# First edge layer of a graph network: VectorE's order, and scatter-adds one group later

## The reference

```python
h  = relu(layernorm(x))
Wh = h @ W + b
Wr, Wc = Wh[row], Wh[col]                    # row = src, col = dst
dot = sum(Wr * Wc);  nr, nc = norms of Wr, Wc
sim = dot / max(nr * nc, EPS)
base = adj_v * sc * (row != col)
prop_pos = segment_sum((base * relu(sim))[:, None] * Wc, row)
prop_neg = segment_sum((base * -relu(-sim))[:, None] * Wc, row)
x = x + scale * (c0 * prop_pos + c1 * prop_neg + c2 * Wh)
```

## Time and profile before

| what | us |
|---|---|
| three runs | 2419.44, 2421.32, 2427.26 (median 2421.32) |
| the profiled execution | 2421.7 |
| its span | 2419.1 |
| GpSimd busy | 1689.1 (70%) |
| TensorE busy | 1563.3 (65%) |
| VectorE busy | 1546.1 (64%) |
| ScalarE busy | 864.6 (36%) |

### The profile page before, as it was taken

One profiled execution on the slowest core, in us unless ns is written; L12 is line 12 of the kernel. 1 busy time (PEld: TensorE's weight loads), 2 busy tenths in 40 slices (PEclk: granted clock), 3 DMA queues, 4 the chain that ended last, 5 costly groups with the idle time before them and its releaser, 6 DMA issues. The chain is left out here.

```text
span 2419.1 us, 57388 instructions
## 1 busy us (share of the span) xinstructions
PE 1563.3 (65%) x16004; PEld 1340.3 (55%) x16004; DVE 1546.1 (64%) x5636; ACT 864.6 (36%) x3093; POOL 1689.1 (70%) x1413
## 2 busy tenths in 40 slices
PE   4886755555455454554555540005999999997998
PEld 2555645545455454554554540005999999994454
DVE  5995655555545555555555551894999999994554
ACT  3773322222222222222222221562333333333665
POOL 2775888888888888888888885746777777751322
PEclk6996555555555555555555555557999999998999
DMA  3775544444444444444444422565555555424664
GB/s 99 251 247 172 114 81 84 75 83 82 76 85 80 78 84 74 85 83 75 85 75 83 84 35 15 181 219 150 125 125 124 126 124 126 123 70 119 187 188 145
DMA packets 342562, 273.11 MB, mean 113 GB/s; under 512 B 144834, under 2 KB 273514, under 8 KB 342484
## 3 DMA queue, kind: packets, MB, share of 16 engines
q1 hardware_dynamic: 259028, 233.22, 33.3%
q0 software_dynamic: 81536, 38.61, 15.1%
q10 hardware_dynamic: 1920, 0.37, 0.1%
HBM read 206.69 MB, written 65.34 MB: 112 GB/s over the span
## 5 line engine op out<-in xcount | busy, mean ns | idle before, releaser
L1111 POOL DMA_INDIRECT x<-e_sums,e_to x392 | 622.7, 1588 | 126.1 <-issue 118.6
L1346 PE MATMUL bank<-e_parts,e_same 128*128 128x64 bf16 x2940 | 172.8, 241 | 579.9 <-DVE e_parts L1205 579.9
L1298 PE MATMUL bank<-e_window,e_onehot 128*128 128x64 f32 x2352 | 525.3, 422 | 16.5 <-DMA e_window<-wh 16.5
L1298 PEld LDWEIGHTS bank<-e_window,e_onehot 128*128 128x128 f32 x2352 | 511.8, 332 | 16.9 <-issue 16.8
L1096 POOL DMA_INDIRECT e_ends<-wh,e_ids x392 | 419.1, 1069 | 132.7 <-issue 101.2
L1346 PEld LDWEIGHTS bank<-e_parts,e_same 128*128 128x128 bf16 x2940 | 159.4, 129 | 595.9 <-issue 595.9
L823 POOL DMA_INDIRECT e_near_source<-h,e_near_ids x392 | 394.9, 1007 | 129.0 <-issue 90.2
L1244 ACT ACTIVATE e_sq<-e_ends 128x64 f32<-128x64 f32 x784 | 188.7, 242 | 680.0 <-DMA e_ends<-wh,e_ids 679.9
L1169 DVE SCALAR_TENSOR_TENSOR e_prod<-e_ends 128x64 f32<-128x64 f32 x392 | 65.5, 222 | 363.4 <-DMA e_ends<-wh,e_ids 363.4
L933 PE MATMUL bank<-e_near_to_edge,e_near_window 128*64 128x128 f32 x2352 | 154.5, 282 | 176.3 <-DMA e_near_window<-h 176.3
L933 PEld LDWEIGHTS bank<-e_near_to_edge,e_near_window 128*64 128x64 f32 x2352 | 130.8, 140 | 182.4 <-DVE e_near_to_edge L844 176.7
(11 more groups left out here) (150 smaller groups left out, 2857.7 us busy)
## 6 DMA issues: line engine op xcount, KB each, us to landing
e_window<-wh SPq DMA_DIRECT2D x392, 96.0 KB
e_near_window<-h SPq DMA_DIRECT2D x392, 96.0 KB
e_owners<-ends SPq DMA_DIRECT2D x98, 256.0 KB, 3.0
n_x<-x SPq DMA_DIRECT2D x98, 256.0 KB, 3.1
n_x<-in_x_dram SPq DMA_DIRECT2D x49, 256.0 KB, 2.8
wh<-n_wh SPq DMA_DIRECT2D x49, 256.0 KB, 2.0
x<-n_x SPq DMA_DIRECT2D x49, 256.0 KB, 2.3
e_rel<-rel SPq DMA_DIRECT2D x98, 128.0 KB, 3.3
```

Source lines behind the costliest of these rows:

```text
L1111: pool.indirect_dma_start(out=added_tab, out_offset=bass.IndirectOffsetOnAxis(ap=t.to[s][:, j:j + 1], axis=0), in_=t.sums[s][:, j, :], in_ ...
L1298: last = nc.tensor.matmul(bank[s % 2][:, j * D:(j + 1) * D], onehot, window, start=w == 0, stop=w == WK - 1)
L1346: last = nc.tensor.matmul(bank[6 + s % 2][:, i * D:(i + 1) * D], t.same[s][:, same_block(j, i), :], t.parts[s][:, part, j, :], start=j == ...
```

## The change

Three lists of parts are written in another order; nothing else is touched. No instruction is added, dropped or resized.

```diff
@@ edge_pool
-    rounds_of_blocks(pool, [(0, gather), (-3, scatter)], ESLOTS, GROUPS)
+    rounds_of_blocks(pool, [(0, gather), (-4 if layer == 0 else -3, scatter)], ESLOTS, GROUPS)
@@ edge_vector
     if layer == 0:
-        parts = [(-3, leave), (0, ahead), (-3, low), (-1, match), (-2, compare), (-2, address), (-2, weigh)]
+        parts = [(-2, compare), (-3, leave), (0, ahead), (-3, low), (-2, address), (-2, weigh), (-1, match)]
@@ edge_scalar
     if layer == 0:
-        parts = [(-3, mid), (-2, norms), (-3, sums)] + [(-1, found)] * near + [(-2, high)]
+        parts = [(-2, norms), (-3, mid)] + [(-1, found)] * near + [(-2, high), (-3, sums)]
```

## The result

The changed kernel took 2439.38 us (median of four runs, 2436.16 to 2440.51) against 2423.68 (2419.44 to 2427.26) for the kernel before in the same comparison: a ratio of 1.0058, 95% interval 1.0039 to 1.0077. It is slower by 0.6%. Repeated later under the label e13_after_again it was 1.0082 [1.0060, 1.0104]. The predicted range of 2398 to 2452 holds the time, but its likeliest case, 2423, is not what happened: the time lies between that and rival B.

The account below looks back on a forecast made before the run. GpSimd's issuing was taken to bound the first edge layer. Loss of 0.55 against 0.58 us a group gave -2.8 us over 94 groups; with ends +1.9 and +2.2, +1.3 on 2421.3: 2423 us, range 2398 to 2452.

Parts of the forecast that it names:

- rival B: Comparisons hit the fourth gather in every round: 0.88 us lost a group, 2454 us; chance 0.31 with milder forms and C.
- three ways to move it: VectorE or ScalarE order changes time only at the layer's ends, by making GpSimd wait, or through issue length.
- Step 1: Layer start: five gather groups precede the first scatter, the fifth waiting for ids; +1.9 us once.
- Step 2: Layer end: five groups left instead of four, so one more wait for a scatter to land; +2.2 us.
- Step 3: VectorE's address step L1217 newly waits for a scatter of its own round to land; nobody delayed, price nothing.
- Step 4: One-hots move from the gathers onto the second scatter's tail and third's head; 0.35 us a group.
- Step 5: Comparisons move near the fourth gather and next first scatter, some groups hit; 0.15 us a group, bounds 0 and 0.5.
- Step 6: ScalarE's new order (norms first, then mid, found, high, sums) costs nothing, since it waits mostly for gathers.
- A: Phases fall well, gathers clear: 0.2 to 0.4 us lost a group, 2399 us; chance 0.32 with milder forms.
- C: L1217's wait makes VectorE late for GpSimd if landings take 5 us longer; 94 us per microsecond beyond; chance 0.02.
- D: Only the layer's ends change, steady loss stays 0.58 us a group: +4.1 us; chance 0.37 together with the forecast.
- The rule on the port: Skill's exclusive VectorE-GpSimd lock: each one-hot blocks GpSimd 1.27 us a group wherever placed; trace supports blocking, not full length.

Follow-up runs that it names:

- e13_after_again: The changed kernel, unaltered, measured again in a later comparison: 2441.12 us, ratio 1.0082 to the kernel before.
- e4: The changed kernel with VectorE's comparisons moved ahead of the address step: ratio 0.9966 to the kernel before, on another chip; first edge layer 1279.8 us.
- e11: As e4, but with scatter-adds three groups back, as in the kernel before: 2399.20 us, ratio 0.9907.
- e2: The changed kernel's VectorE and ScalarE order alone, scatter-adds three groups back as in the kernel before: 2414.90 us, ratio 0.9966.
- e7: The changed kernel with the one-hots' columns taken in a strided order (stride 256): ratio 1.0167 to the kernel before, on another chip.
- e9: As e2, with the one-hots' columns taken in a strided order (stride 256): ratio 1.0006 to the kernel before, on another chip.
- e6: The changed kernel with four idle VectorE copies ahead of the copy of `ef` and the comparisons: ratio 0.9912 to the kernel before, on another chip.
- e1: The kernel before with only its scatter-adds one group further back, VectorE's and ScalarE's order unchanged: 2413.06 us, ratio 0.9977.

## Why the prediction was right or wrong

**What bounds the layer** (GpSimd's issuing, three ways to move it): right. In every kernel GpSimd's waits between 300 and 1400 us have a mean of 0.305 us, whatever releaser is named, and the layer's length follows the sum of the eight issues.

**Step 1, the start:** +1.9 predicted, +1.0 measured in waits. **Step 2, the end:** four waits, of 2.52, 2.38, 2.37 and 2.41, as predicted; they come to +1.9 where +2.2 was taken.

**Step 3, L1217:** right in what it costs by itself and in its place: VectorE stands 4.8 us each time, until 1.68 behind the scatter's end, within the 1.5 to 2.3 given. ScalarE now waits for the messages (432.5 us in the waits above), and GpSimd does not wait for ScalarE.

**Step 4, the one-hots: a wrong cause, with the right scatters.** The second and third scatters did lengthen, by 1.714 - 1.58 = 0.13 and 1.650 - 1.555 = 0.10, so 0.23 and not 0.35. But the one-hots cost them nothing. The split and the low part hold the two starts, and the prediction had the low part (with the messages) at 0.05 and the split at nothing. The one-hots were also placed half a scatter off: they are over before the third scatter starts. Rows 6 had been misread in the same way. The scatters at 896.38 and 251.49 were put down to one-hots, and what lies over their starts is the messages and the split, on VectorE in the kernel before:

```profile
896.14 0.42 DVE L1187 SCALAR_TENSOR_TENSOR e_msgs<-e_ends,e_small 128x256 f32<-128x256 f32 x1
...
251.38 0.42 DVE L1200 SCALAR_TENSOR_TENSOR e_left<-e_msgs,e_parts 128x256 f32<-128x256 f32 x1 [0.47 <-ACT e_parts L1262]
```

So "scatters lengthen under the one-hots" seemed to come true by luck. The reading of rows 5, one-hots over a gather's start, holds.

**Step 5, the comparisons: the term that was mis-sized.** 0.15 us was taken, 0.40 was measured (1.342 - 0.945). The mechanism was the one named, and so was the price of a hit (0.48 by rows 5; 0.51 in the round shown). The failed step is "landing times vary by a tenth or more, so some groups get one and some the other". They do vary, from 1.53 to 1.85, but with a standard deviation of 0.06, and nearly all lie on one side of the switch; both loops are locked to the same scatter: GpSimd's fourth gather comes 4.15 behind its end, VectorE's widest comparison 1.68 + 2.27 = 3.95 behind it (0.20 ahead of the gather in the mean). The gather itself starts 0.10 later than the 4.04 of the prediction's count, since the first two gathers take 1.01 and 0.97 and not 0.94. 79 rounds of 83 get the hit. This is rival B at the gather, at nearly its full rate; its "landing of 1.6 us down" was a tenth or two strict, for the hit ends where the comparison starts 0.10 ahead of the gather, 4.05 behind the scatter, and that is a landing of 4.05 - 2.27 = 1.78. Rival B itself says that the place is "the same in every round", and yet the forecast took a mixture. With one place for all rounds the term is 0 or 0.4 to 0.5. Which of the two, the rows of before left open: their landings of 1.5 to 2.3 lie on both sides of 1.78.

**The base of the sum.** The loss of before was put at 0.58 us a group, from four gathers of 0.94. In kernels where nothing of VectorE's wide work lies over the gathers' starts (e4, e11) the first takes 1.014 and the second 0.968: they are longer behind a scatter anyway. By the sum over places, before loses 4.286 - 3.87 = 0.41 at its gathers and 0.05 at its scatters, 0.47; after loses 0.40 and 0.25, 0.65. So there was 0.11 less to win than I had thought, and 0.65 rather than 0.55 was lost. +0.18 x 94 = 17 instead of -2.8 us.

**Step 6:** ScalarE's order costs nothing; in e2, which has it, the layer is shorter than before.

**The rivals:** B is what happened at the fourth gather, where 0.40 was lost as a mean over all rounds, for its 0.48. Its other terms, 0.35 for the one-hots and 0.05 for the low part, stand for 0.23 that the split and the low part cost. By its count 0.88 is lost, by the measured places 0.65; it gave 2454, and 2439 was measured. A (2399) is not this kernel, but the phases that it describes exist: e11, with 2399.20, has them, through an order and not through luck. C did not occur. D gives the ends only, 2.9 of the layer's 18.8.

**The rule on the port.** The table of the switch shows this: a comparison that starts less than a tenth ahead of a gather lies over it and costs it nothing, and one that starts 0.15 ahead delays it by 0.5 us. The Trainium skill, SBUF — State Buffer, section "SBUF: two separate sides", has VectorE and GpSimd share a port pair under an exclusive lock. The blocking agrees with it, and so does its length where an operation is under way at an issue's start: the gather ends 0.82 behind the comparison's end in all 79 rounds. A loss of the whole instruction wherever it stands does not agree. Plain one-hots inside a scatter cost it nothing, and e11 and after run the same instructions and differ by 0.48 us a round.

## What to carry to other kernels

Where two engines meet at a short moment of each other's instructions, a mean over many rounds is a mean of hits and misses: look at the places in the round one by one, and at what is under way at the start of each. The widest operation near an issue need not be the one that holds it; check that the issue's end keeps a fixed distance from the suspect's end. A wait that delays nobody can still cost time, because it locks the phase (the place in the round) of all that is queued behind it; work out that one phase, and do not average over phases that a lock excludes. To move the wide work of one engine away, put it behind a releaser that leaves the widest clearance (here: behind the gathered rows, ahead of the step that waits for the landing), and try a few idle copies first: they show in one run on which side of the switch one is.

## What the runs showed of the hardware

The issue of an indirect DMA on GpSimd is held by a wide operation of VectorE (128x256 or more) that is under way at its start, until that operation is over. It has to have begun some 0.10 us ahead of a gather's start, or 0.04 ahead of the second scatter's. In after a held gather ends 0.82 us behind the comparison's end (79 rounds), a held scatter 1.43 to 1.46 behind that of the split or the low part (64 rounds each). A comparison begun 0.10 to 0.30 us ahead of the fourth gather so makes 0.94 into 1.27 to 1.47, and one begun later costs nothing. Inside a scatter plain one-hots cost nothing (1.58 to 1.60 in 19 rounds of after), while one-hots with strided columns hold it until 0.12 behind their end (82 scatters of e7, 2.141 in the mean), though not in every place (e9). A gather behind four scatters takes 1.01 and the next 0.97, against 0.94 for the third, with no wide operation over their starts. The instruction that waits for a scatter's landing starts 1.68 us behind the end of its issue in after (1.53 to 1.85), 1.90 in e6 and 2.11 in e1. And VectorE pays too: the three one-hots take 1.27 us in rows 5, 1.34 in e11's round, and 1.69 in after's, inside the second scatter.
